# Six of sixteen attention units: probabilities transposed in blocks through DRAM, logits issued two units ahead

## What is computed

```
xn = layernorm(ctx); ln = layernorm(layernorm(x))
q = ln @ Wq                                   # 16 heads of 64
k, v = split([xn ; ln] @ Wkv)                 # 1024 + 64 = 1088 keys per batch
sim = rmsnorm(q) * 64**-0.5 @ rmsnorm(k).T    # masked keys get -max
out = softmax(sim) @ v                        # per batch and head
x = x + concat(out) @ Wout + bout
```

## Time and profile before

| | |
|---|---|
| median of 3 executions | 223.56 us |
| the profiled execution, and its span from first to last instruction | 222.66 us, 220.9 us |
| PE, DVE, ACT, POOL busy (share of the span) | 212.8 (96%), 158.5 (72%), 148.9 (67%), 79.7 (36%) us |
| mean granted TensorE clock | 0.999 |
| chain that ended last, by engine | PE 69%, DVE 11%, ACT 9%, POOL 5%, issue 5% |

### The profile page before, as it was taken

How to read it: one execution, slowest core, us unless ns; L and a number is a source line. 1 busy time by engine, 2 the same in 40 slices (tenths; PEclk the granted TensorE clock), 3 DMA queues, 4 the chain that set the end, 5 groups by cost and what they waited for, 6 DMA issues and landing times.

```text
span 220.9 us, 4126 instructions
## 1 busy us (share of the span) xinstructions
PE 212.8 (96%) x1394; PEld 185.0 (84%) x1394; DVE 158.5 (72%) x362; ACT 148.9 (67%) x329; POOL 79.7 (36%) x129
## 2 busy tenths in 40 slices
PE   6899999999999999999999999999999999999984
PEld 6566878887788898989898889999999997899873
DVE  3889999998968989888878557676877631413531
ACT  4778799979895776858583867876777555315161
POOL 4488887861593846626151300000000010000300
PEclk9999999999999999999999999999999999999999
DMA  6480135200000234152325999720000000000000
GB/s 188 146 307 27 49 119 192 71 27 0 24 3 0 98 97 154 44 185 95 95 95 157 376 397 195 172 48 3 1 0 3 1 0 0 3 0 3 0 0 24
DMA packets 18500, 18.78 MB, mean 85 GB/s; under 512 B 7176, under 2 KB 16560, under 8 KB 18224
## 3 DMA queue, kind: packets, MB, share of 16 engines
q1 hardware_dynamic: 17928, 16.95, 24.5%
q10 hardware_dynamic: 552, 1.58, 2.0%
HBM read 15.51 MB, written 2.75 MB: 83 GB/s over the span
## 4 chain that ended last, share of the span: by engine, by line
PE 69%; DVE 11%; ACT 9%; POOL 5%; issue 5%; POOLq 0%; ACTq 0%; DVEq 0%
PE banks L1440 20%; PE banks L1268 10%; PE banks L1377 9%; PE banks L1337 8%; PE banks L1585 5%; PE banks L1463 4%; PE banks L1470 4%; DVE small L973 3%; DVE sk L985 2%; PE banks L1380 2%; PE banks L1512 2%; PE banks L1612 2%; POOL xn L535 1%; POOL xg L528 1%; ACT knT L687 1%
## 5 line engine op out<-in xcount | busy, mean ns | idle before, releaser
L1016 DVE TENSOR_TENSOR ptl<-banks,pth 128x512 fp32r<-128x512 f32 (+1 forms) x48 | 26.1, 554 | 17.6 <-ACT pth L729 17.3
L1440 PE MATMUL banks<-xnh,pth 128*128 128x256 f32 x128 | 37.6, 294 | 0.0
L1440 PE MATMUL banks<-xnh,ptl 128*128 128x256 f32 x128 | 36.1, 282 | 0.0
L1440 PE MATMUL banks<-xnl,pth 128*128 128x256 f32 x128 | 36.1, 282 | 0.0
L564 POOL TENSOR_TENSOR small<-small 128x16 f32<-128x16 f32 x7 | 20.4, 2915 | 27.3 <-DVE small L980 27.3
L729 ACT ACTIVATE pth<-banks 128x512 fp32r<-128x512 f32 (+1 forms) x48 | 23.7, 494 | 9.5 <-PE banks L1268 8.5
L669 ACT ACTIVATE sk<-banks 128x512 f32<-128x512 f32 x36 | 20.8, 601 | 11.5 <-PE banks L1337 11.0
L973 DVE TENSOR_REDUCE small<-sk 128x8 f32<-128x512 f32 x36 | 23.5, 678 | 3.6 <-ACT sk L669 3.6
L545 POOL COPY sp<-sp 128x64 f32<-128x64 f32 x16 | 4.3, 266 | 59.9 <-ACT sp L708 59.9
L985 DVE TENSOR_TENSOR sk<-banks,small 128x512 f32<-128x512 f32 x36 | 22.9, 679 | 2.7 <-POOL small L564 2.4
L1440 PEld LDWEIGHTS banks<-xnh,pth 128*128 128x128 f32 x128 | 24.4, 191 | 0.5 <-issue 0.4
(11 more groups left out here) (204 smaller groups left out, 474.8 us busy)
## 6 DMA issues: line engine op xcount, KB each, us to landing
knT<-in_L_attn_qkv_kernel SPq DMA_DIRECT2D x1, 3072.0 KB, 12.5
spread<-knT SPq DMA_DIRECT2D x5, 512.0 KB, 2.6
knT<-spread SPq DMA_DIRECT2D x20, 128.0 KB, 2.9
raw<-in_ctx SPq DMA_DIRECT2D x16, 128.0 KB, 2.3
knT<-in_L_xattn_Wq SPq DMA_DIRECT2D x1, 1024.0 KB, 5.7
wv<-in_L_xattn_Wkv ACTq DMA_DIRECT2D x1, 1024.0 KB, 5.9
wout_sb<-in_L_xattn_Wout SPq DMA_DIRECT2D x1, 1024.0 KB, 5.7
knT<-in_L_attn_out_kernel SPq DMA_DIRECT2D x1, 1024.0 KB, 15.9
```

What stands on the lines that cost most here:

```text
L1016: nc.vector.tensor_tensor(ptl[:, j0:j1, :], banks[:, t3_bank(u, c), 0:(j1 - j0) * P].rearrange("p (j r) -> p j r", j=j1 - j0), pth[:, j0:j ...
L1440: nc.tensor.matmul(banks[:, u_bank(u), 0:D], p_[:, j, :], x_, start=(j == 0 and i == 0), stop=False)
```

## The change

- Units 10 to 15 (`SPREAD` = 10): the eight context blocks of the probabilities are no longer transposed on PE. DVE transposes 32 x 32 blocks into `p_blocks` (`prob_blocks`); SP stores them to DRAM (`p_spread`), waits, and loads them in four DMAs into `p_back[u % 2]`, both in the space of batch 0's context, which is free after unit 7. One ACT copy (`spread_high`) and one DVE subtraction (`spread_low`), each 128 x 1024, take the place of two pairs. The latents' block is still transposed on PE.
- `mix` of these units comes in three pieces: `mix_high` (16 matmuls with pth), `mix_low` (8 with ptl) and `mix_latents` (2); the last two of unit u are issued in unit u + 1.
- The logits run two units ahead from unit 7 on, `values` of these units two behind.
- Units 11 to 15 compute their logits in plain float32; their `unit_high` and `unit_low` go.
- All `attended` products now lie in units 14 and 15. `outk` and Wout2 are loaded in four pieces behind the loads of units 10 to 13; the means of `outk` and the transposes of Wout1 and Wout2 on DVE move behind `probs_low(14, 2)`.

```diff
+            for u in range(SPREAD, UNITS):
+                n = u - SPREAD
+                sp.wait_ge(pb_ready, n + 1)
+                sp.dma_start(p_spread[n], p_blocks).then_inc(pb_stored, 16)
+                sp.wait_ge(pb_stored, 16 * (n + 1))
+                if n >= 2:
+                    sp.wait_ge(ptl_ready, split_count(u - 2, 0))
+                for c in range(4):
+                    sp.dma_start(p_back[n % 2][c * QD:(c + 1) * QD, :].rearrange("a (i m) -> a i m", i=4),
+                                 p_spread[n][:, c * D:(c + 1) * D].rearrange("(i a) m -> a i m", i=4)
+                                 ).then_inc(pq_landed[n % 2], 16)
+                if n < 4:
+                    sp.dma_start(outk_sb[:, 2 * n:2 * n + 2, 0:D], outk_v[:, 2 * n:2 * n + 2, :]).then_inc(w_tail["outk"], 16)
...
+            def spread_high(u):
+                n = u - SPREAD
+                act.wait_ge(pq_landed[n % 2], 64 * (n // 2 + 1))
+                if u == SPREAD:
+                    act.wait_ge(u_ps, u)
+                else:
+                    act.wait_ge(mh_ps, n)
+                    act.wait_ge(ptl_ready, split_count(u - 1, 0))
+                nc.scalar.activation(probs_rows(pth), spread_blocks(p_back[n % 2]), ACT.Copy).then_inc(pth_ready, 1)
...
+            for u in range(SPREAD + 1, UNITS - 1):
+                if u - 2 >= SPREAD:
+                    heads_out(u - 2)
+                spread_high(u)
+                if u + 2 < UNITS:
+                    exponentials(u + 2)
+                mix_out(u - 1)
+                probs_high(u, 2)
+                mixT_out(u - 1)
+            u = UNITS - 1
+            heads_out(u - 2)
+            mix_out(u - 1)
+            mixT_out(u - 1)
+            spread_high(u)
+            probs_high(u, 2)
+            heads_out(u - 1)
...
+            def spread_low(u):
+                dve.wait_ge(pth_ready, split_count(u, 0))
+                dve.wait_ge(u_ps, u)
+                nc.vector.tensor_tensor(probs_rows(ptl), spread_blocks(p_back[u % 2]), probs_rows(pth).bitcast(F32),
+                                        ALU.subtract).then_inc(ptl_ready, 1)
+
+            def prob_blocks(u):
+                dve.wait_ge(exp_ready, u + 1)
+                if u == SPREAD:
+                    dve.wait_ge(u_ps, G)
+                else:
+                    dve.wait_ge(pb_stored, 16 * (u - SPREAD))
+                nc.vector.transpose(p_blocks.rearrange("p (j c r) -> p c j r", j=4, r=QD),
+                                    sp2[:, u % 2, 0:J].rearrange("p (c j r) -> p c j r", c=NT, r=QD)).then_inc(pb_ready, 1)
...
+            for u in range(SPREAD, UNITS - 3):
+                logits_max(u + 2)
+                prob_blocks(u + 2)
+                spread_low(u)
+                inverse_sum(u + 2)
+                probs_low(u, 2)
...
+            for u in range(SPREAD + 1, UNITS - 2):
+                probs_transposed(u, 2)
+                if u - 2 >= SPREAD:
+                    values(u - 2)
+                all_logits(u + 2)
+                mix_low(u - 1)
+                mix_latents(u - 1)
+                mix_high(u)
+                mix_transposed(u - 1)
```

More of the change, by code:

```diff
@@ L1139, in _ @@
                     tile_sums(i + 4)
[L1140 to L1151, removed]
+                key_scale(i + 1, 0)
+                key_scale(i + 1, 1)
+                inverse_sum(u + 1)
+            probs_low(G - 1, 0)
+            probs_low(G - 1, 1)
+            logits_max(G)
+            unit_low(G + 1)
+            probs_low(G - 1, 2)
+            unit_low(G + 2)
+            logits_max(G + 1)
+            inverse_sum(G)
+            probs_low(G, 0)
+            probs_low(G, 1)
+            logits_max(G + 2)
+            probs_low(G, 2)
+            inverse_sum(G + 1)
+            prob_blocks(G + 2)
+            inverse_sum(G + 2)
+            probs_low(G + 1, 0)
+            probs_low(G + 1, 1)
+            logits_max(G + 3)
+            probs_low(G + 1, 2)
+            prob_blocks(G + 3)
+            inverse_sum(G + 3)
+            for u in range(SPREAD, UNITS - 3):
[4 more added lines that the diff above has]
+                probs_low(u, 2)
+            u = UNITS - 3
+            logits_max(u + 2)
+            spread_low(u)
+            prob_blocks(u + 2)
+            probs_low(u, 2)
+            inverse_sum(u + 2)
+            spread_low(u + 1)
+            probs_low(u + 1, 2)
+            for j in range(0, G, 2):
+                out_means(j)
+            dve.wait_ge(w_tail["ffn_a"], 128)
+            for there, here in w1T_parts:
+                nc.vector.transpose(here, there).then_inc(w1T_ready, 1)
+            spread_low(u + 2)
+            probs_low(u + 2, 2)
             dve.wait_ge(dchain, own[0])
@@ L1512, in attended, with all_logits @@
                 return nc.tensor.matmul(banks[:, 2, 0:D], oT[:, g, :], wout_sb[:, g, :], start=(g == 0), stop=(g == G - 1))
-            for u in range(UNITS - 1):
+            def all_logits(u):
+                for part in range(3):
+                    logits(u, part)
+            for u in range(G):
                 i = ITEMS_A + u
@@ L1517, in _ @@
                     probs_transposed(0, 0)
-                    for part in range(3):
-                        logits(1, part)
+                    all_logits(1)
                     probs_transposed(0, 1)
@@ L1553, in _ @@
-            probs_transposed(u, 1)
+                if u < G - 1:
+                    mix(u)
+            mix(G - 1, (0, 1))
+            all_logits(G + 1)
+            mix(G - 1, (2,))
+            for u in range(G, SPREAD):
+                for c in range(3):
+                    probs_transposed(u, c)
+                mix_transposed(u - 1)
+                all_logits(u + 2)
+                values(u - 1)
+                mix(u)
+            u = SPREAD
+            probs_transposed(u, 2)
+            mix_transposed(u - 1)
@@ new lines, in _ @@
+            mix_low(u - 1)
+            mix_latents(u - 1)
+            attended(0)
+            attended(1)
+            mix_high(u)
+            mix_transposed(u - 1)
+            u = UNITS - 1
+            probs_transposed(u, 2)
+            values(u - 2)
+            mix_low(u - 1)
+            mix_latents(u - 1)
+            for g in range(2, 5):
+                attended(g)
+            pe.wait_ge(xb_ready, 1)
+            nc.tensor.matmul(banks[:, 2, 0:D], ident[:, :], xb[:, :], start=False, stop=False)
```

173 lines of the change are left out of this document (118 added, 55 removed).

## The result

The changed kernel took 227.82 us (median of 4 runs, 227.45 to 227.99), the kernel before 223.53 us (223.19 to 224.33) beside it: ratio 1.0185, 95% interval 1.0155 to 1.0215, so 4.3 us slower. Forecast were 225.9 us and a range of 222.4 to 228.6. The sign and the range held; the loss is almost twice the forecast of +2.33.

A forecast was written before the change was run, and what follows sets the result against it. PE bound units 8 to 14; after the change, handoffs make it wait. PE work -2.88, new waits +5.64, old slack -0.43 give +2.33 us, put on the median of 223.56: 225.9 us, range 222.4 to 228.6.

The forecast's parts named there:

- signs of being wrong: PE busy 10 of 10 between 150 and 180, spread_high waiting on DMA, logits under 6.2 us apart, clock under 1.00 before 200.
- The new loop: Units 11 to 13: handoffs in series take 6.64 us between logits, against 5.95 us of PE work; chance 0.62.
- The schedule: Step-by-step waits from the logits of unit 9 to mix_out(15): 5.64 us of new waits, mix_out(15) at 187.15.
- What it adds elsewhere: New work off PE: prob_blocks 1.24 us, spread_low 1.22, spread_high 1.05, and a trip through DRAM of 6.8 us.
- Units 11 to 15 gain 5 x 0.48 = 2.40 us: PE work added by plain logits, 1.84 us a unit against 1.36 for parts 0 and 1 of split logits.
- Costed at nothing: Weight pieces behind the loads of units 10 to 13, moved DVE weight work, dropped splits and the DRAM trip add no time.
- The trip of 6.8 us is covered: Unit 11's blocks land at 153.6, before ACT can use them at 154.57; other units have 1.2 to 2.8 us to spare.
- late-trip rival: Units 10 to 15: the trip through DRAM binds from 9.6 us on; about 230 us, chance 0.08.
- PE as the bound: mix_out and mixT_out results come in time, so only PE's sum of -2.88 us counts; 220.7 us, chance 0.14.
- half of the waits: Neighbouring steps of an engine overlap, so only half of the added waits show; 223.1 us, chance 0.14.
- The clock: A granted clock under 1.00 before 200 us; chance 0.02, no time given.
- T(15): Start of the last part of the logits of unit 15, forecast at 167.71 us.

The follow-up runs named there:

- e1: The changed kernel with the outk pieces issued behind the qkv load and the Wout2 pieces behind Win1, as before the change; 225.84 us, ratio 1.0119.
- e7: The kernel before with only the logits of units 11 to 15 in plain float32 on unsplit keys; 224.74 us, ratio 1.0067.
- e11: The changed kernel with a second buffer for the blocked probabilities, units taking turns; 227.33 us, ratio 1.0169.
- e5: The changed kernel without the DRAM trip of units 12 to 15, which reuse the blocks of units 10 and 11 (wrong result); 226.08 us, ratio 1.0141.
- e3: e1 with DVE running spread_low ahead of prob_blocks in the passes of units 10 to 12; 225.70 us, ratio 1.0119.
- e9: The changed kernel with ACT, PE, DVE and last passes reordered, weights behind unit 15's loads, and stores cut in halves; 223.86 us, ratio 1.0040.
- e10: e9 with the keys of units 12 to 15 split again, GpSimd making the low parts; 223.86 us, ratio 1.0016.

## Why the prediction was right in sign and short in size

The main mechanism is right: the loop of handoffs took PE's place as the bound. The number owes something to the width of the range. 227.82 us lies above the range that the prediction gives for the loop alone (224.4 to 227.4) and inside the whole one (222.4 to 228.6), which also covers parts of rivals; and of its signs of being wrong one came, `spread_high` waiting on DMA. Two causes added up, the loop and the late trip, and the forecast had only the first.

- **"The new loop ... 6.64 us"** holds: 6.73 in e1, where nothing else stands in the chain. Its pieces, from e1's rows: 0.37 to the maximum, 1.33, 1.32, 0.53, 0.48 and 0.44 up to `values`, 0.55 for `values` (0.45 forecast, a length that was read where PE was already running) and 1.72 for two parts of logits (1.84 forecast). Two errors of a tenth cancel.
- **The schedule** holds. Logits' last parts of units 14 and 15 start at 161.36 and 168.10 in e1; forecast were 161.07 and 167.71, and that stretch (from the logits of unit 9) began 0.29 us later in this profile (131.53) than the forecast's 131.24. `mix_high` of unit 15 waits for ACT, and the table load stands ahead of `mix_out(15)`, as written.
- **"What it adds elsewhere", the three new operations on DVE and ACT**, hold to 0.03 us.
- **"Units 11 to 15 gain 5 x 0.48 = 2.40 us"** was mis-sized: e7 shows 0.32 a unit, 1.6 us, and 1.4 in its median. The 1.36 us of the split parts came from a unit of the other batch, whose keys lie unblocked; in unit 14 of the kernel before the two parts add 0.70 us each to the chain of waits:

```profile
172.13 0.70 PE banks L1377 x3
...
173.49 0.70 PE banks L1377 x3
```

That is 1.40 us, against 1.72 for plain parts in e7 (1.84 assumed), so 0.32. In the loop only the length of the logits counts, so this moved the forecast little.

- **"Costed at nothing" is the step that failed**, in two of its sentences. "The pieces of `outk` and Wout2 follow the loads ... in an idle queue": the queue was idle in the trace of before, and the change itself filled the DMA engines to a share of 0.6; SP's issuing of the pieces alone held up the stores of units 13 and 14 by 1.0 us each. "The trip of 6.8 us is covered ... 1.2 to 2.8 us to spare": the 2.62 us were a store alone; behind loads and pieces the stores of units 12 to 14 took 3.1, 5.3 and 3.9 us (168.01 to 171.96), each late one delaying the next, and `spread_high` of these units waited 1.25 to 2.40 us. e1 removed 1.5 us of the 4.3 by moving the pieces alone (medians over before 4.3 and 2.75). The late-trip rival named the place, but at 230 us and a chance of 0.08 had it too dear and too unlikely.
- The single block buffer, not in the prediction, added at most some tenths (e11).
- **PE as the bound (220.7)** and **half of the waits** fell: the loop was as long as added up (6.73 us). **The clock** stayed at 1.00.

What is left open: e1 and e5 lie 0.4 to 0.6 us above the forecast's +2.33, about what the intervals allow. In their profiles, counted from the start of the stretch (131.53 and 131.87, forecast 131.24), T(15) comes only 0.1 us late and `mix_out(15)` 0.5 us (187.91 and 188.24, forecast 187.15), so most of it lies in the passes behind T(15); which term there holds it is not settled. No run separates the two things that the pieces do, holding up SP's issuing and lengthening the stores. And whether loads from another engine's queue would shorten the trip was not tried.

## What to carry to other kernels

When PE stops being the bound, add up the handoffs of the loop that remains; that sum of rows was right to 0.1 us a round, while PE's own sum, on the ground that the other engines have room, gave 220.7 us, 5 us under e1. Price a transfer by the queue as the change will fill it, not as the old trace shows it: what else is in flight when it is issued, and what waits behind it. Work that "only follows in the queue" is not free when the next round's first transfer follows it.

## What the runs showed of the hardware that was not expected

- A store of 512 KB took 2.7 us with nothing in flight, 2.9 to 4.8 us shortly behind four loads (units 14 and 13 of e3), and 3.9 and 5.3 us right behind loads and weight pieces (units 14 and 13 of the change); half of it took 2.1 us (e9). What sets the place in these ranges is not shown. The Trainium skill, "SBUF — State Buffer", section "The DMA setup-cost knee", gives a fit of 2 us and a part by size at 436 GB/s, which as an estimate by that page makes 3.2 us for the whole and 2.6 us for the half; alone (the whole) and with the other half beside it, both measure 0.5 us less.
- DVE's rounding copy of 128 x 1024 to float32r took 0.69 us in e10, ACT's 1.05.
- The four matmuls of `values` hold PE for 0.55 us when PE has just waited for `uT` (e1, 165.83 to 166.38), and 0.44 to 0.45 us in an unbroken sequence (e9, 164.85 to 165.29; the earlier trace rows).
